# Routing stage of a fused transformer kernel: chunk 0's logits, choice and slots first on each engine, the row statistics of chunk 3 behind them

## The chip, the cores and the metric

The kernel runs on one NeuronCore of a Trainium2 chip. TensorE (PE; PEld are its weight loads), VectorE (DVE), ScalarE (ACT), GpSimd (POOL) and the DMA queues of SyncE (SP) run lists of instructions of their own and meet at semaphores. The metric is the device time of one execution in microseconds (us); three runs of the kernel before gave 1239.8 to 1245.31, median 1242.03.

## What is computed

```python
x = x + _layernorm(_L0_attn_ref(_layernorm(x, axis=-1), ...), axis=-1)   # attention, x is (8, 256, 256)
x = x + _layernorm(_L0_ffn_ref(_layernorm(x, axis=-1), ...), axis=-1)    # mixture of experts
x = x + _layernorm(_L1_attn_ref(_layernorm(x, axis=-1), ...), axis=-1)   # state space layer
x = x + _layernorm(_L1_ffn_ref(_layernorm(x, axis=-1), ...), axis=-1)    # dense layers

def _L0_ffn_ref(x, router_w, router_bias, wg, wu, wd, swg, swu, swd):
    logits = flat @ router_w                                     # 2048 tokens, 64 experts
    _, topk_idx = jax.lax.top_k(logits + router_bias, 4)
    ...
    routed = jnp.einsum('ne,nef,efd->nd', comb, g * u, wd)       # four experts a token
    shared = jnp.einsum('nsh,shd->nd', sg * su, swd)             # two experts that see every token
    return (routed + shared).reshape(b, t, d)
```

The change lies in the first part of the second line: the normalised rows, the logits, the choice of four experts and the places ("slots") to which each token's row is sent.

## The kernel before

The 2048 tokens lie in 16 tiles of 128, and four tiles make a chunk: chunks 0 to 3. The attention stage ends with `y`, the attention's output. For chunks 0 and 1 it has itself normalised `y`, added it to `x`, and written the normalised `rows`. For chunks 2 and 3 this is left to the routing stage (`stage_route`, from line 869), which runs these lists:

- VectorE (from line 1280): `statistics(src, kind, g)` takes mean and variance of four tiles. `low_parts(g)` makes the low half of the transposed rows, `choose(g)` ranks the logits and marks four experts, `tables(n)` sums how many rows each expert has, `find_slots(g)` writes `slots`, which releases the scatters of chunk g. `add(g)` adds the normalised `y` to `x`. `product(n)` and `low(n)` belong to step n of the shared experts, 16 steps, four for each chunk.
- GpSimd (from line 950): a "deviation" is a power of -0.5 and a product, by `spread`, with `deviations(kind, g)` for y or x. Then 64 indirect DMAs, one for each tile and choice, send rows of 128 tokens from `rows` to `slots_in` in DRAM (line 971). Two may be in flight (`IN_FLIGHT`): number n waits until n - 2 has landed. `BEFORE_ROWS` says ahead of which number a deviation is done.
- TensorE (from line 1058): `turn(g)` transposes rows, `score(g)` makes logits (24 products of 64 columns), `place_chunk(g)` counts and ranks once `choose(g)` is done. `up(n)` and `down(n)` are the shared experts' products; the second half of `up(n)` waits for `product(n - 1)`, `down(n)` for `low(n)`. Chunk 0's four steps come first, then `turn(2)`, which needs the accumulators back.
- ScalarE (from line 1131): `high_parts(0)`, `high_parts(1)`, `scale_y(2)`, `scale_y(3)`, `step(0)`, `step(1)`, `fill_rows(2)`, `step(2)`, `fill_rows(3)`, `step(3)`, `take(0)`. `scale_y(g)` waits for y's deviation of chunk g, `fill_rows(g)` for x's; `step(n)` makes the gate (a SiLU) of step n and rounds its product; `take(0)` empties the accumulators (`y_out`).
- SyncE (line 941): waits until all scatters have landed and loads the rows of the first experts from `slots_in`, on which the next stage begins.

The waits on deviations go by number: `rstd_ready` counts in the order of `NORM_ORDER`, (y, 2), (y, 3), (x, 2), (x, 3). The orders are written out by hand.

Of the kernel before, what the change touches and what calls it, by code (L numbers as in the profile page):

```python
# [24 lines left out]
FE, TOPK = 64, 4  # L25
# [6 lines left out]
NCH = TOK // CHUNK  # L32
TPC = CHUNK // P
# [51 lines left out]
def linker(eng, sem):  # L85

    n = [0]

    def link(ins):
        n[0] += 1  # L90
        ins.then_inc(sem, 1)
        eng.wait_ge(sem, n[0])

    return link
# [15 lines left out]
def flat(ap):  # L110
    return ap.rearrange("p a b -> p (a b)")
# [304 lines left out]
OF_Y, OF_X = range(NORMS)  # L416
# [5 lines left out]
EARLY_NORMS = 2  # L422
# [21 lines left out]
def spread(nc, link, norms, kind, tiles):  # L444

    part = slice(tiles.start, tiles.stop)
    rstd = norms["rstd"][:, kind, part]
    link(nc.gpsimd.tensor_tensor(rstd, norms["var"][:, kind, part], norms["power"][:], ALU.pow))
    return nc.gpsimd.tensor_tensor(norms["shift"][:, kind, part], norms["negmean"][:, kind, part], rstd, ALU.mult)
# [360 lines left out]
PARTIES = PARTY[-1] + 1  # L810
N_SEEN, N_OVER, N_LIMIT, N_BASE = range(4)
NORM_ORDER = [(OF_Y, 2), (OF_Y, 3), (OF_X, 2), (OF_X, 3)]
BEFORE_ROWS = {4: 2, 8: 3}
SLOT_TILES = NE + OVER
SLOT_ROWS = SLOT_TILES * P
BLANK = 8
# [52 lines left out]
def stage_route(chip, x, rows, norms, xh, xl, y, ident, xs, t, ahead, router, ins):  # L869
# [10 lines left out]
    with ExitStack() as ctx:  # L880
# [45 lines left out]
        slots_ready, scattered = chip.sem("slots_ready"), [chip.kept_sem("scattered") for _ in range(IN_FLIGHT)]  # L926
# [4 lines left out]
        def tiles(g):  # L931
            return slice(g * TPC, (g + 1) * TPC)
# [5 lines left out]
        def normed(kind, g):  # L938
            return NORM_ORDER.index((kind, g)) + 1

        with nc.Block() as block:
            @block.sync
            def _(sp):
                for q in range(AHEAD):
                    load_experts(sp, ahead, ins, q, ahead["w_loaded"][q])
                for done in scattered:
                    sp.wait_ge(done, NT * TOPK // IN_FLIGHT * 16)
                for g in range(DEEP):
                    load_quad(sp, xs, ahead, g)

            @block.gpsimd
            def _(pool):
                chip.clear_old()
                link = linker(pool, pool_link)

                def deviations(kind, g):
                    pool.wait_ge(var_ready, normed(kind, g))
                    spread(nc, link, norms, kind, range(g * TPC, (g + 1) * TPC)).then_inc(rstd_ready, 1)

                for g in range(EARLY_NORMS, NCH):  # L960
                    deviations(OF_Y, g)
                for g in range(NCH):
                    pool.wait_ge(slots_ready, g + 1)
                    for i in range(g * TPC, (g + 1) * TPC):
                        for k in range(TOPK):
                            n = i * TOPK + k
                            if n in BEFORE_ROWS:
                                deviations(OF_X, BEFORE_ROWS[n])
                            if n >= IN_FLIGHT:
                                pool.wait_ge(scattered[n % IN_FLIGHT], n // IN_FLIGHT * 16)  # L970
                            nc.gpsimd.indirect_dma_start(  # L971
                                out=xs[:, :], out_offset=bass.IndirectOffsetOnAxis(slots[:, i, k:k + 1], 0),
                                in_=rows[:, i, :], in_offset=None).then_inc(scattered[n % IN_FLIGHT], 16)

            @block.tensor
            def _(pe):
                def turn(g):
                    for b in (2 * g, 2 * g + 1):
                        if g >= EARLY_NORMS:
                            pe.wait_ge(xn_ready, b - 2 * EARLY_NORMS + 1)  # L980
                        if b >= len(turned):
                            pe.wait_ge(lo_ready, b - len(turned) + 1)
                        for n in range(2):
                            for k in range(KD):
                                last = nc.tensor.transpose(turned[b % len(turned)][:, k, n * P:(n + 1) * P],
                                                           rows[:, 2 * b + n, k * P:(k + 1) * P], ident[:])
                        last.then_inc(xn_turned, 1)
# [3 lines left out]
                def score(g):  # L991
                    if g >= 2:
                        pe.wait_ge(logits_out, g - 1)
                    for i in range(TPC):
                        if i % 2 == 0:
                            pe.wait_ge(lo_ready, 2 * g + i // 2 + 1)
                        t0 = (g * TPC + i) * P
                        for m, (a, w, k) in enumerate(parts):
                            last = nc.tensor.matmul(logits[g % 2][:, i, :], a[:, k, t0:t0 + P], w[:, k, :],
                                                    start=(m == 0), stop=(m == len(parts) - 1))  # L1000
                    last.then_inc(logits_done, 1)
# [23 lines left out]
                def place_chunk(g):  # L1025
                    pe.wait_ge(chosen_done, g + 1)
                    count(g)
                    rank(g)
# [28 lines left out]
                    last.then_inc(down_done, 1)  # L1057

                turn(0)
                turn(1)  # L1060
                score(0)
                place_chunk(0)
                score(1)
                pe.wait_ge(logits_out, 1)
# [89 lines left out]
            def _(dve):  # L1154
                link = linker(dve, chain)

                def statistics(src, kind, g):
                    for i in range(g * TPC, (g + 1) * TPC):
                        last = nc.vector.bn_stats(norms["stats"][:, kind, i, :], src[:, i, :])
                    link(last)  # L1160
                    measure(nc, link, norms, kind, range(g * TPC, (g + 1) * TPC)).then_inc(var_ready, 1)

                def add(g):
                    dve.wait_ge(y_scaled, g - EARLY_NORMS + 1)
                    link(nc.vector.tensor_tensor(flat(x[:, tiles(g), :]), flat(x[:, tiles(g), :]),
                                                 flat(y[:, tiles(g), :]), ALU.add))

                def low_parts(g):
                    for b in range(2 * g, 2 * g + 2):
                        dve.wait_ge(hi_ready, b + 1)  # L1170
                        nc.vector.tensor_tensor(xl[:, :, b * S:(b + 1) * S], turned[b % len(turned)],
                                                xh[:, :, b * S:(b + 1) * S].bitcast(F32),
                                                ALU.subtract).then_inc(lo_ready, 1)

                def choose(g):
                    dve.wait_ge(logits_done, g + 1)
                    link(nc.vector.tensor_tensor(ranked[:, tiles(g), 0:NE], logits[g % 2],
                                                 bias[:].unsqueeze(1).broadcast_to([P, TPC, NE]), ALU.add))
                    nc.vector.tensor_copy(logit[:, tiles(g), :], logits[g % 2]).then_inc(logits_out, 1)
                    for i in range(g * TPC, (g + 1) * TPC):  # L1180
                        last = nc.vector.max(best[:, i, :], ranked[:, i, :])
                    link(last)
                    for i in range(g * TPC, (g + 1) * TPC):
                        last = nc.vector.match_replace(left[:, i, :], best[:, i, :], ranked[:, i, :], -BIG)
                    link(last)
                    nc.vector.tensor_tensor(chosen[:, tiles(g), :], ranked[:, tiles(g), 0:NE], left[:, tiles(g), 0:NE],
                                            ALU.not_equal).then_inc(chosen_done, 1)
# [73 lines left out]
                def product(n):  # L1261
                    dve.wait_ge(silu_done, n + 1)
                    dve.wait_ge(up_done, n + 1)
                    if n >= 2:
                        dve.wait_ge(lo_done, n - 1)
                        dve.wait_ge(hi_done, n - 1)
                    nc.vector.tensor_tensor(prod[:, n % 2, :], gate[:, n % 2, :], pu[:], ALU.mult).then_inc(prod_done, 1)
# [9 lines left out]
                    product(n)  # L1277
                    low(n)

                statistics(y, OF_Y, 2)  # L1280
                nc.vector.memset(ranked[:, :, NE:], BIG)
                link(nc.vector.memset(scan[:], 0.0))
                set_tables()
                low_parts(0)
                low_parts(1)
                statistics(y, OF_Y, 3)
                choose(0)
                add(2)
                tables(0)
                find_slots(0)  # L1290
                choose(1)
                product(0)
                statistics(x, OF_X, 2)
                low(0)
# [1712 lines left out]
```

## Time and profile before

| | before |
|---|---|
| median of three runs | 1242.03 us |
| profiled execution | 1239.46 us |
| its span | 1237.6 us |
| busy of the span: PE, DVE, ACT, POOL | 1106.0, 869.7, 637.7, 378.7 us |
| routing stage | about 220 to 346 us |

The span is measured from the first instruction to the last; the profiled execution's own time has 1.9 us more around it. The chain of waits that the profile follows back from the last instruction covers only the last part of the kernel, so for the routing stage the timelines of the engines have to be read.

### The profile page before, as it was taken

The page shows a single profiled execution, that of the slowest core. Times are in us where ns is not written, and L with a number is a line of the kernel's source. Part 1 is how long each engine was busy: PE and PEld are TensorE (multiplying, and loading weights), DVE is VectorE, ACT ScalarE, POOL GpSimd, SP SyncE. Part 2 cuts the span into 40 slices and gives each one's busy share as a digit, 9 for nine tenths or more (in the row PEclk, how much of TensorE's full clock was granted, in tenths as well). Part 3 has the DMA queues.
Part 4 walks back from the last instruction along what each step waited for, and adds up shares of the span by engine and source line. Part 5 has one row for each costly group of instructions (what it writes and reads, how often), then busy time and mean ns, then how long its engine had stood idle before and what let it go on. Part 6 is the DMA issues. An engine that isn't in the chain of part 4 may idle for free. (4 is left out here: it accounts for less than half of the span.)

```text
span 1237.6 us, 31648 instructions
## 1 busy us (share of the span) xinstructions
PE 1106.0 (89%) x12161; PEld 909.0 (73%) x12161; DVE 869.7 (70%) x2188; ACT 637.7 (52%) x1449; POOL 378.7 (31%) x545
## 2 busy tenths in 40 slices
PE   6779998788989994777699999999999999999996
PEld 5646775677778994555467888888888888888896
DVE  6767896867946678776476677667766776664675
ACT  4644545233333784666545555555455545553665
POOL 3521222266700065761263036102610262000121
PEclk9979999678999997778899999999999999999998
DMA  6838883222289896551523243223342342232001
GB/s 173 248 123 218 237 219 138 117 80 90 86 329 419 294 316 206 165 184 77 144 83 95 87 125 108 87 87 121 113 157 91 112 124 87 87 104 87 5 18 52
DMA packets 77986, 176.17 MB, mean 142 GB/s; under 512 B 12614, under 2 KB 26182, under 8 KB 75270
## 3 DMA queue, kind: packets, MB, share of 16 engines
q1 hardware_dynamic: 71564, 157.09, 39.1%
q0 software_dynamic: 6272, 17.05, 4.5%
q8 instruction: 97, 1.59, 0.5%
q14 instruction: 53, 0.43, 0.1%
HBM read 112.82 MB, written 61.08 MB: 141 GB/s over the span
## 5 line engine op out<-in xcount | busy, mean ns | idle before, releaser
L2395 ACT ACTIVATE decay<-masked,negcum 128x128 f32<-128x128 f32 x512 | 163.1, 391 | 102.1 <-DVE mixT L2459 102.1
L2303 PE MATMUL joint<-xh,w_high 128*128 128x512 f32 x512 | 209.2, 409 | 2.0 <-POOL wl L2239 2.0
L2303 PE MATMUL joint<-xl,w_high 128*128 128x512 f32 x512 | 200.2, 391 | 0.0
L2303 PE MATMUL joint<-xh,wl 128*128 128x512 f32 x512 | 199.9, 390 | 0.0
L2507 DVE COPY cT<-joint 128x512 f32<-128x512 f32 x128 | 88.3, 689 | 85.8 <-PE joint L2303 85.4
L2413 ACT ACTIVATE bT<-joint 128x512 f32<-128x512 f32 x128 | 76.6, 599 | 130.4 <-PE joint L2303 130.4
L2459 DVE TENSOR_TENSOR mixT<-pcb,decay 128x512 f32<-128x512 f32 x128 | 82.4, 685 | 53.8 <-PE pcb L2319 53.8
L2236 POOL TENSOR_TENSOR w_high<-w_in,none 128x512 fp32r<-128x512 f32 x32 | 34.7, 1084 | 262.3 <-DMA w_in<-in_w_bc 253.2
L2303 PEld LDWEIGHTS joint<-xh,w_high 128*128 128x128 f32 x512 | 96.2, 188 | 23.7 <-POOL wl L2239 2.4
L2303 PEld LDWEIGHTS joint<-xh,wl 128*128 128x128 f32 x512 | 96.1, 188 | 20.7
L2303 PEld LDWEIGHTS joint<-xl,w_high 128*128 128x128 f32 x512 | 96.3, 188 | 17.0
L2449 DVE TENSOR_TENSOR masked<-cumrow,mask 128x512 f32<-128x512 f32 x128 | 101.9, 796 | 0.1
L699 ACT ACTIVATE probT<-pst 128x384 f32<-128x384 f32 x128 | 60.2, 490 | 65.2 <-PE pst L630 61.9
L2319 PEld LDWEIGHTS pcb<-cT,bT 128*32 128x32 f32 x4096 | 79.4, 110 | 11.7 <-issue 11.7
L2319 PE MATMUL pcb<-cT,bT 128*32 128x128 f32 (+3 forms) x4096 | 84.7, 234 | 0.0
L971 POOL DMA_INDIRECT slots_in<-rows,slots x64 | 66.3, 1036 | 41.8 <-DMA slots_in<-rows,slots 20.4
L2468 DVE TENSOR_TENSOR cS<-cT,grown 128x256 f32<-128x256 f32 x128 | 62.4, 488 | 13.4 <-ACT grown L2400 1.3
L1602 DVE TENSOR_TENSOR rows<-gate,pgu 64x512 f32<-64x512 f32 x64 | 44.2, 691 | 26.4 <-ACT gate L1557 25.4
L738 DVE CUSTOM_DVE_ANT_0 masked<-ps,reach 128x128 f32<-128x128 f32 x128 | 36.7, 286 | 24.5 <-PE ps L614 23.3
L740 DVE CUSTOM_DVE_ANT_0 masked<-ps,reach 128x256 f32<-128x256 f32 x128 | 53.7, 419 | 0.0
L2400 ACT ACTIVATE grown<-cumrow 128x256 f32<-128x256 f32 x128 | 51.6, 403 | 0.0
L2251 POOL COPY y<-val 32x128 f32<-32x128 f32 x128 | 43.2, 337 | 7.6
(369 smaller groups left out, 2698.7 us busy)
## 6 DMA issues: line engine op xcount, KB each, us to landing
cumrow<-ssm_cum SPq DMA_DIRECT2D x128, 256.0 KB, 3.3
slots_in<-blank SPq DMA_DIRECT2D x16, 1024.0 KB, 5.3
rows<-slots_in SPq DMA_DIRECT2D x32, 512.0 KB, 5.9
slots_out<-spare SPq DMA_DIRECT2D x32, 512.0 KB, 4.8
weights<-in_expert_quads SPq DMA_DIRECT2D x16, 768.0 KB, 9.0
w_in<-in_w_bc SPq DMA_DIRECT2D x32, 256.0 KB, 3.7
qk_parts<-parts SPq DMA_DIRECT2D x32, 192.0 KB, 2.8
stack<-qk_parts SPq DMA_DIRECT2D x32, 192.0 KB, 5.1
```

The lines of the kernel that those rows point to most:

```text
L699: nc.scalar.activation(probT[:, n % HELD, :], pst[n % T_BANKS][:, 0:3 * P], ACT.Exp).then_inc(exped, 1)
L740: nc.vector.tensor_tensor_reduce(dst[:, P:3 * P], src[:, P:3 * P], reach[:], accum_out=highest[:, u % 2, j, 1:2], **form).then_inc(maxed, 1)
L971: nc.gpsimd.indirect_dma_start(out=xs[:, :], out_offset=bass.IndirectOffsetOnAxis(slots[:, i, k:k + 1], 0), in_=rows[:, i, :], in_offset=N ...
L2303: last = nc.tensor.matmul(bank[:], w[:, j, col:col + P], a[:, k, c * CHUNK:(c + 1) * CHUNK], start=(m == 0), stop=(m == len(parts) - 1))
L2319: last = nc.tensor.matmul(pcb[n % 2][at:at + KEY, reach], bT[:, n % B_BUFS, keys], cT[:, n % 2, reach], start=True, stop=True, skip_group_ ...
L2395: last = nc.scalar.activation(decay[:, n % 2, o], masked[:, n % 2, o], ACT.Exp, bias=negcum[:, c * TPC + i, head:head + 1])
L2400: nc.scalar.activation(grown[:, n % 2, :, :], row[:, :, P:S], ACT.Exp).then_inc(grown_out, 1)
L2413: nc.scalar.activation(bT[:, n % B_BUFS, :], pbT[:], ACT.Copy).then_inc(b_out, 1)
L2449: nc.vector.tensor_tensor(masked[:, n % 2, :].rearrange("p (q l) -> p q l", l=S), cumrow[:, n % CUMS, :].rearrange("p (q l) -> p q l", l=S ...
L2459: nc.vector.tensor_tensor(mixT[:, n % KEEP, :], pcb[n % 2][:], decay[:, n % 2, :], ALU.mult).then_inc(mix_out, 1)
L2468: nc.vector.tensor_tensor(cS[:, n % KEEP, :, :], second, grown[:, n % 2, :, :], ALU.mult).then_inc(c_scaled, 1)
L2507: nc.vector.tensor_copy(cT[:, n % 2, :], pcT[:]).then_inc(c_out, 1)
```

## The change

It alters the order of work in the routing stage on three engines, and nothing else.

- VectorE: the memsets and tables come first, then `low_parts(0)`, `statistics(y, 2)`, `choose(0)`, `low_parts(1)`, `tables(0)`, `find_slots(0)`; then `statistics(y, 3)`, `choose(1)`, `add(2)`, and from `product(0)` on the list is as before.
- TensorE: `score(0)` comes ahead of `turn(1)`.
- GpSimd: y's deviation of chunk 2 is done before the wait for chunk 0's slots, y's of chunk 3 ahead of scatter 4, x's of chunks 2 and 3 ahead of scatters 8 and 12 (before: y's both first, x's ahead of 4 and 8).

ScalarE's and SyncE's lists are as before.

```diff
-BEFORE_ROWS = {4: 2, 8: 3}
+BEFORE_ROWS = {0: (OF_Y, 2), 4: (OF_Y, 3), 8: (OF_X, 2), 12: (OF_X, 3)}
...
-                for g in range(EARLY_NORMS, NCH):
-                    deviations(OF_Y, g)
                 for g in range(NCH):
-                    pool.wait_ge(slots_ready, g + 1)
                     for i in range(g * TPC, (g + 1) * TPC):
                         for k in range(TOPK):
                             n = i * TOPK + k
                             if n in BEFORE_ROWS:
-                                deviations(OF_X, BEFORE_ROWS[n])
+                                deviations(*BEFORE_ROWS[n])
+                            if n % (TPC * TOPK) == 0:
+                                pool.wait_ge(slots_ready, g + 1)
                             if n >= IN_FLIGHT:
...
                 turn(0)
+                score(0)
                 turn(1)
-                score(0)
                 place_chunk(0)
...
-                statistics(y, OF_Y, 2)
                 nc.vector.memset(ranked[:, :, NE:], BIG)
                 link(nc.vector.memset(scan[:], 0.0))
                 set_tables()
                 low_parts(0)
+                statistics(y, OF_Y, 2)
+                choose(0)
                 low_parts(1)
-                statistics(y, OF_Y, 3)
-                choose(0)
-                add(2)
                 tables(0)
                 find_slots(0)
+                statistics(y, OF_Y, 3)
                 choose(1)
+                add(2)
                 product(0)
```

## Rows read from the trace of the kernel before

**Rows 1.** GpSimd's timeline: start us, us, engine, line, what, [idle before <-releaser].
```profile
229.47 0.20 POOL L449 TENSOR_TENSOR norm_shift<-norm_negmean,norm_rstd 128x4 f32<-128x4 f32 x1
241.67 1.22 POOL L971 DMA_INDIRECT slots_in<-rows,slots  x1 [12.01 <-DVE slots L1251]
...
246.91 1.26 POOL L448 TENSOR_TENSOR norm_rstd<-norm_var,norm_power 128x4 f32<-128x4 f32 x1
248.25 0.21 POOL L449 TENSOR_TENSOR norm_shift<-norm_negmean,norm_rstd 128x4 f32<-128x4 f32 x1
...
289.34 1.05 POOL L971 DMA_INDIRECT slots_in<-rows,slots  x1 [0.30 <-DMA slots_in<-rows,slots]
293.08 0.95 POOL L971 DMA_INDIRECT slots_in<-rows,slots  x1 [2.69 <-DVE slots L1251]
...
339.82 0.96 POOL L971 DMA_INDIRECT slots_in<-rows,slots  x1 [0.44 <-DMA slots_in<-rows,slots]
```

**Rows 2.** SyncE's timeline at the end of the stage.
```profile
342.31 6.26 SPq L862 DMA_DIRECT2D rows<-slots_in  x4
```

**Rows 3.** VectorE's timeline, from the stage's start to `low(3)`.
```profile
220.70 1.41 DVE L1159 BATCH_NORM_STATS2 norm_stats<-y 128x6 f32<-128x256 f32 x4 [0.33 <-PEq L523]
...
222.75 0.11 DVE L1281 MEMSET ranked<- 128x64 f32 x1
...
223.55 1.29 DVE L1171 TENSOR_TENSOR xl<-acc,xh 128x512 fp32r<-128x512 f32 x2
...
230.91 1.22 DVE L1165 TENSOR_TENSOR x<-x,y 128x1024 f32<-128x1024 f32 x1
232.16 0.22 DVE L1198 TENSOR_TENSOR table<-table,counts 128x64 f32<-128x64 f32 x1
...
241.28 0.42 DVE L1177 TENSOR_TENSOR ranked<-pg,router_bias 128x256 f32<-128x256 f32 x1
...
243.98 0.68 DVE L1267 TENSOR_TENSOR prod<-gate,pu 128x512 f32<-128x512 f32 x1
...
249.23 0.69 DVE L1267 TENSOR_TENSOR prod<-gate,pu 128x512 f32<-128x512 f32 x1 [0.84 <-PE pu L1034]
...
253.43 0.69 DVE L1267 TENSOR_TENSOR prod<-gate,pu 128x512 f32<-128x512 f32 x1 [0.92 <-ACT gate L1125]
...
259.71 0.68 DVE L1267 TENSOR_TENSOR prod<-gate,pu 128x512 f32<-128x512 f32 x1
...
263.23 0.69 DVE L1273 TENSOR_TENSOR hl<-prod,hh 128x512 fp32r<-128x512 f32 x1
```

**Rows 4.** ScalarE's timeline.
```profile
221.37 1.08 ACT L1096 ACTIVATE xh<-acc 128x512 fp32r<-128x512 f32 x2 [9.17 <-PE acc L985]
...
239.86 0.60 ACT L1125 ACTIVATE gate<-pg 128x512 f32<-128x512 f32 x1 [6.79 <-PE pg L1034]
...
250.49 2.07 ACT L454 ACTIVATE rows<-x,norm_shift,norm_rstd 128x256 f32<-128x256 f32 x4
...
306.06 1.28 ACT L1125 ACT_TABLE_LOAD   x1
307.35 0.60 ACT L1125 ACTIVATE gate<-pg 128x512 f32<-128x512 f32 x1
```

**Rows 5.** Busy time by stretch; behind POOL's: granted clock, DMA share, GB/s.
```profile
224.00:227.00 3.00, 2.71 (x25) 2.71 (x25) 2.82 (x7) 2.02 (x5) 0.16 (x1) 1.00 1.01 418
227.00:232.00 5.00, 1.87 (x14) 1.67 (x14) 4.83 (x24) 2.83 (x7) 1.20 (x2) 0.50 0.58 242
```

**Rows 6.** TensorE's timeline: products of the logits.
```profile
224.70 0.28 PE L999 MATMUL pu<-router_wh,xh 128*128 128x64 f32 x1
...
226.82 0.28 PE L999 MATMUL pu<-router_wl,xh 128*128 128x64 f32 x1
...
231.79 0.40 PE L999 MATMUL pg<-router_wh,xh 128*128 128x64 f32 x1
...
236.70 0.40 PE L999 MATMUL pg<-router_wh,xl 128*128 128x64 f32 x1
```

## The prediction

> **What bounds the kernel now.** I read four views of the routing stage, in this order. First GpSimd's timeline. The 64 row scatters are the stage's last work: number 0 starts at 241.67 us, number 31 at 289.34, then GpSimd idles 2.69 us for the slots of chunk 2, and numbers 32 to 63 run from 293.08 to 339.82, a pitch of 1.51 us [rows 1]. SyncE waits for the last landing and loads the first expert rows at 342.31 [rows 2]. So the end hangs on when chunk 2's slots are written, not on when the first scatter starts: chunks 0 and 1 have idle time behind them.
>
> Then, what makes chunk 2's slots late. TensorE must give the accumulators of chunk 0's shared experts back (`y_out`) before `turn(2)`, so the chain runs back over `down(3)` to the DVE step `low(3)`, at 263.23 [rows 3]. Behind it the order is fixed: `low(3)`, `down(3)`, `take(0)`, `turn(2)`, `score(2)`, `choose(2)`, `choose(3)`, `tables(2)`, `find_slots(2)`, 32 scatters. A shift of `low(3)` is a shift of the stage's end, one for one.
>
> Last, what `low(3)` hangs on. In front of it VectorE works nearly without a pause from 220.70: the pauses marked are 0.84 us before `product(1)` and 0.92 us before `product(2)` [rows 3]. ScalarE is idle for much of it; it takes the first gate at 239.86 after waiting 6.79 us for TensorE [rows 4]. TensorE's clock is at its high level (1.00, 2.4 GHz) to 227 us and at the low one (0.50, 1.2 GHz) behind it [rows 5].
>
> **The change part by part.** The instructions are the same ones; none is added. Only orders change, on three engines. ScalarE's order is not touched, and there the price lies: its list still says `scale_y(2)`, `scale_y(3)`, `step(0)`. `scale_y(3)` waits for chunk 3's y power, which so far came at 229.5 + 0.2, long before the gate [rows 1]. I follow the new times.
>
> *VectorE's front.* `statistics(y, 2)` costs 2.05 us (220.70 to 222.75), the memsets and `set_tables` 0.80 (to 223.55) [rows 3]. Now the memsets go first, to 221.50. `low_parts(0)` needs ScalarE's first `xh`, 221.37 + 0.60 [rows 4], so it starts at 222.05 and, at 0.61 each (as `low_parts` ran), ends at 223.25. `statistics(y, 2)` then lasts to 225.3. Its power is done beside `choose(0)` on an idle GpSimd, so `scale_y(2)` and `add(2)` are never late.
>
> *TensorE's front.* `score(0)` starts after the first low part, 222.75. It is 24 products of 64 columns. At the high clock their pitch is 0.112 us (224.70 to 226.82 in 19 steps), at the low one 0.2135 (231.79 to 236.70 in 23) [rows 6]. Bounds, with the last one's own length: all high 222.75 + 23 x 0.112 + 0.28 = 225.6; all low 222.75 + 23 x 0.2135 + 0.40 = 228.1. The clock fell once while `score(0)` ran, although 12 transposes and 4 more preceded the fall; now 8 transposes and a pause of 1 us do, and narrow products. I take the fall after the first six products: 222.75 + 6 x 0.112 + 17 x 0.2135 + 0.40, the logits are there at 227.5. That is nearer to the low end, because the engine does less in front of it than in the rows where the high level was kept.
>
> *Choice and slots of chunk 0.* `choose` costs 2.70 us (241.28 to 243.98), `tables(0)` and `find_slots(0)` 9.12 together (232.16 to 241.28) [rows 3]. `choose(0)` ends at 230.2; `low_parts(1)` follows, 1.2 us, to 231.4, and covers `place_chunk(0)` on TensorE as `add(2)` did (1.25 us, 230.91 to 232.16). If that cover were gone the wait would be about 1 us. Slots: 231.4 + 9.1 = 240.5 instead of 241.28. So the first scatter is 0.8 us earlier, at 240.9 (2.7 us earlier if the clock holds).
>
> *The power of y 3 behind four scatters.* `statistics(y, 3)` now follows the slots: 240.5 to 242.55. Then `choose(1)` to 245.25 and `add(2)` to 246.5. GpSimd meets `deviations(y, 3)` as number 4 is due. From number 0 to that point is 246.91 - 241.67 = 5.24 us, power and shift take 1.55 (246.91 to 248.25 + 0.21) [rows 1]: 240.9 + 5.24 + 1.55 = 247.7. Then ScalarE: `scale_y(3)` 2.07 us as the four of `fill_rows(2)` take, the table load 1.29 (306.06 to 307.35), the gate and the step to VectorE 0.63 [rows 4]. Together 251.7. `product(0)` was at 243.98 [rows 3]: it is **7.7 us later**, and VectorE, ready at 246.5, idles 5.2 us. Queued behind the wait on ScalarE are `step(0)`, `step(1)`, `fill_rows(2)` and all that follows; behind VectorE's wait `statistics(x, 2)` and everything to `low(3)`; TensorE's `up(1)` stops halfway, since its second half waits for `product(0)`.
>
> On the table load a rule and a row differ. The row of the switch after the exponential shows 1.28 us, and the gate starts 0.01 us behind it [rows 4]. The Trainium skill ("ScalarE: Activation LUTs", What ACT_TABLE_LOAD costs) adds a drain and gives 2.66 us for each switch; by it the sum would be 1.4 us more. The row is this case's, and I go by it.
>
> *What is won back.* Between `product(0)` and `product(1)` 0.84 us of waiting for TensorE falls away, since `up(1)`'s gate half is long done: 4.4 us instead of 5.25, so `product(1)` is at 256.1, 6.9 late [rows 3]. The 0.92 us ahead of `product(2)` stay, because ScalarE still puts `fill_rows(2)` (2.07) between: 4.2 us on, 260.3. The x powers come at scatter 8 and 12 instead of 4 and 8. x 2 is measured at 251.7 + 0.6 + 2.05 = 254.3, when GpSimd has made four scatters at 1.51 behind 247.7 (253.7); its power is done at 255.9, before `fill_rows(2)` can start at some 257.4. x 3 is due four scatters later, at 261.9, and done at 263.5; `fill_rows(3)` then lasts to 265.6 and the gate of `step(3)` to 266.2, while `product(3)` is due at 260.3 + 6.3 = 266.6 (253.43 to 259.71): hidden, with 0.4 us left. If four scatters took 2 us more, it would cost 1.6.
>
> *Chunks 0 and 1 on GpSimd.* One power more between scatters is 1.5 us in a queue that must wait for chunk 1's and chunk 2's slots anyway: nothing.
>
> *Sum.* From `product(2)` to `low(3)` nothing changes (9.8 us, 253.43 to 263.23), so `low(3)` is at 270.1, **6.9 us late**, and so is the stage. The stages behind it are the same. The profiled execution took 1239.46 us for a span of 1237.6, and would become 1246.4. It lay 2.6 us under the median of 1242.03; on the median I forecast 1248.9. A half per cent, 6.2 us, is about what a measurement of this kernel can tell from no change.
>
> **The rivals.**
> A. *The clock holds through `score(0)`.* Then the logits are there at 225.6, the slots at 225.6 + 2.7 + 1.2 + 9.1 = 238.6, and all behind them is 1.9 us earlier than in the sum: `low(3)` 5.0 us late, 1247.0. For it: all 8 transposes and the first 20 products ran high in the kernel before [rows 6]. Against: the same narrow products then fell to the low level, and the work ahead of them is a third less. The Trainium skill ("TensorE: Matmul & The Clock Gate", HAM oscillation) says that pauses between bursts lose the high clock, which speaks for the forecast and against A; the fall behind 227 us in the trace [rows 5] agrees.
> B. *TensorE becomes late.* It idles while VectorE waits; if it is at the low clock in `up(1)` to `up(2)`, 18 wide products and 12 of `down(0)` at twice their time put `product(2)` 1 to 2.7 us later. With 2.5: 1251.4.
> C. *Faster: the scatter queue is the bound from the first one on.* Then the first scatter's lead of 2.7 us less the extra power's 1.5 is won: 1240.8, and with that power hidden in a pause 1239.3. It needs slots of chunk 2 before scatter 31 ends. Against it stands GpSimd's wait of 2.69 us [rows 1]; it decides only if `low(3)` is not held up by the gate, as it would with y 3's power before the first scatter.
> D. *The stall is absorbed:* 3 us or less are left of it, because `low(3)` to chunk 2's slots runs at another mix of clock levels (the scores at the high one throughout are worth 1.7 us) and ScalarE's part is shorter: 1244.5.
>
> **How the numbers follow.** Forecast 0.50, A 0.26, B 0.12, C 0.04, D 0.08. Predicted time 1248.9. Range 1244.5 to 1252.5: from D's value to B's with 1 us for the median of a few runs. Slower by over 0.5% (beyond 1248.2): 0.7 of the forecast, a quarter of A, B nearly all, 0.54. Within 0.5%: the rest of the forecast and of A, D, half of C, 0.43. Faster by over 0.5% needs more than C gives as I price it: 0.03.
>
> **What would show it.** In the new trace: first scatter at 239 to 241; y 3's power at 244 to 246, behind four scatters; ScalarE idle up to it, then `scale_y`, the table load and the gate in one row, the gate's idle naming no TensorE; VectorE's wait of about 5 us ahead of `product(0)`, put down to ScalarE; `low(3)` near 270; GpSimd's wait ahead of scatter 32 grown from 2.7 us to 5 or more; SyncE's first load near 349. The prediction is wrong if the gate comes before 248, if `low(3)` moves and scatter 32 does not, or if scatter 32 moves and the last landing does not.

## The result, and the profile after

| | before | changed |
|---|---|---|
| median of 7 runs each | 1243.06 us | 1251.36 us (1248.25 to 1254.32) |
| ratio to before | 1 | 1.0065, 95% interval 1.0049 to 1.0081 |
| profiled execution, its span | 1239.46, 1237.6 | 1252.56, 1250.6 |

The change costs 8.3 us by the medians. The forecast was 6.9 us more and a time of 1248.9.

The routing stage of the changed execution begins 1.04 us earlier (VectorE's first instruction at 219.66, before at 220.70, [rows 3]), so all comparisons of places below count from the stage's start. VectorE's timeline of the changed kernel answers [rows 3]; the columns are start, duration, engine, line, operation, and in brackets the idle time ahead and what ended it.

```profile
219.66 0.11 DVE L1279 MEMSET ranked<- 128x64 f32 x1 [0.37 <-PEq L523]
...
221.44 1.47 DVE L1170 TENSOR_TENSOR xl<-acc,xh 128x512 fp32r<-128x512 f32 x2 [1.01 <-ACT xh L1095]
...
227.55 0.42 DVE L1176 TENSOR_TENSOR ranked<-pu,router_bias 128x256 f32<-128x256 f32 x1 [2.64 <-PE pu L998]
...
245.29 1.22 DVE L1164 TENSOR_TENSOR x<-x,y 128x1024 f32<-128x1024 f32 x1
251.81 0.69 DVE L1266 TENSOR_TENSOR prod<-gate,pu 128x512 f32<-128x512 f32 x1 [5.30 <-issue]
...
256.27 0.69 DVE L1266 TENSOR_TENSOR prod<-gate,pu 128x512 f32<-128x512 f32 x1
...
260.53 0.69 DVE L1266 TENSOR_TENSOR prod<-gate,pu 128x512 f32<-128x512 f32 x1 [0.98 <-ACT gate L1124]
...
266.88 0.69 DVE L1266 TENSOR_TENSOR prod<-gate,pu 128x512 f32<-128x512 f32 x1 [0.23 <-ACT gate L1124]
...
270.41 0.69 DVE L1272 TENSOR_TENSOR hl<-prod,hh 128x512 fp32r<-128x512 f32 x1
```

The reader is to see the 5.30 us ahead of the first product. The profile calls it "issue", but ScalarE's timeline says what it is:

```profile
229.82 2.06 ACT L454 ACTIVATE y<-y,norm_shift,norm_rstd 128x256 f32<-128x256 f32 x4
247.74 2.07 ACT L454 ACTIVATE y<-y,norm_shift,norm_rstd 128x256 f32<-128x256 f32 x4 [15.86 <-POOL norm_shift L449]
249.83 1.28 ACT L1124 ACT_TABLE_LOAD   x1
251.13 0.60 ACT L1124 ACTIVATE gate<-pg 128x512 f32<-128x512 f32 x1
```

ScalarE stands still for 15.86 us, released by GpSimd; `scale_y(3)`, the table load and the gate follow without a gap, and 0.08 us behind the gate VectorE goes on. The gate itself waits for nothing: TensorE's last product for it ended at 239.2, some 12 us before the gate. GpSimd's timeline, which answers [rows 1], has the power that is waited for, behind four scatters:

```profile
240.97 1.22 POOL L970 DMA_INDIRECT slots_in<-rows,slots  x1 [14.69 <-DVE slots L1250]
...
246.24 1.19 POOL L448 TENSOR_TENSOR norm_rstd<-norm_var,norm_power 128x4 f32<-128x4 f32 x1
247.50 0.21 POOL L449 TENSOR_TENSOR norm_shift<-norm_negmean,norm_rstd 128x4 f32<-128x4 f32 x1
...
293.54 0.96 POOL L970 DMA_INDIRECT slots_in<-rows,slots  x1 [0.30 <-issue]
300.69 0.96 POOL L970 DMA_INDIRECT slots_in<-rows,slots  x1 [6.20 <-DVE slots L1250]
...
348.75 0.96 POOL L970 DMA_INDIRECT slots_in<-rows,slots  x1 [0.30 <-DMA slots_in<-rows,slots]
```

and SyncE's, which answers [rows 2]:

```profile
351.24 6.34 SPq L862 DMA_DIRECT2D rows<-slots_in  x4
```

Where the time went, counted from each stage's start (start to place, in us):

| place | before | changed | later by | forecast |
|---|---|---|---|---|
| first scatter | 20.97 | 21.31 | 0.34 | -0.8 |
| `product(0)` | 23.28 | 32.15 | 8.87 | 7.7 |
| `product(1)` | 28.53 | 36.61 | 8.08 | 6.9 |
| `low(3)` | 42.53 | 50.75 | 8.22 | 6.9 |
| scatter 32 | 72.38 | 81.03 | 8.65 | 6.9 |
| SyncE's first load | 121.61 | 131.58 | 9.97 | 6.9 |

From the start of the kernel the load is 8.93 us later, since the stage began 1.04 earlier. The span of this execution is 13.0 us longer than that of before, which is 4.7 more than the medians differ: the further stages add 4.1 in this pair of executions. The main loop of the state space stage, whose code is unchanged, starts 12.8 us later (SyncE's `w_in` loads at 607.53 and 620.31), so nearly all of that came up ahead of it. I didn't follow it further. The medians, of seven executions each, differ by 8.3 us only, so I don't count it to the change.

### The profile page after: what moved, and what is told of

Read it like the earlier page. It is cut to its first block and busy times, and to the rows that moved or that the text cites. A ratio compares the mean times of both kernels' runs of the same rounds, so it can differ in the third digit from the quotient of the medians.

```text
span 1250.6 us, 31647 instructions
## 1 busy us (share of the span) xinstructions
PE 1114.1 (89%) x12161; PEld 915.2 (73%) x12161; DVE 870.3 (70%) x2188; ACT 637.7 (51%) x1449; POOL 383.1 (31%) x545
## 5 line engine op out<-in xcount | busy, mean ns | idle before, releaser
L1481 PE MATMUL pt<-ident,rows 128*128 128x128 f32 x256 | 37.0, 288 | 10.5 <-PEq L941 6.1
```

## The experiments

All times are medians of runs of the kernel beside runs of the kernel before on the same chip, and the ratio is to those. "Stage" is the time from VectorE's first instruction of the routing stage to TensorE's first transpose of the next (before: 125.66 us), and `low(3)` counts from the same start (before: 42.53); both are of the one profiled execution. Where two runs of the table are compared with each other, the noise given is the 95% interval of the difference of their ratios.

| kernel | median, before beside it | ratio, 95% interval | `low(3)` | stage |
|---|---|---|---|---|
| changed | 1251.36, 1243.06 | 1.0065, 1.0049 to 1.0081 | 50.75 | 135.62 |
| y power at scatter 4, x's at 8 and 12, nothing else | 1252.59, 1243.07 | 1.0083, 1.0065 to 1.0102 | 52.69 | 138.89 |
| y power at scatter 8, x's at 12 and 14, nothing else | 1257.60, 1242.59 | 1.0107, 1.0078 to 1.0135 | 55.93 | 139.35 |
| `score(0)` first, alone | 1248.12, 1243.07 | 1.0046, 1.0029 to 1.0062 | 48.95 | 133.05 |
| changed, `turn(1)` first | 1248.48, 1242.59 | 1.0045, 1.0027 to 1.0063 | 49.03 | 134.85 |
| changed, y power at scatter 2 | 1249.63, 1242.59 | 1.0057, 1.0036 to 1.0077 | 46.96 | 129.50 |
| changed, gate ahead of `scale_y(3)` | 1246.37, 1243.07 | 1.0026, 1.0012 to 1.0041 | 47.05 | 129.15 |
| changed, y 3 measured in the gap | 1244.61, 1243.07 | 1.0015, 1.0001 to 1.0029 | 46.89 | 128.84 |
| the same, x powers at 4 and 8 | 1242.65, 1242.39 | 1.0001, 0.9985 to 1.0018 | 43.93 | 127.58 |
| before, `low(3)` earlier | 1241.68, 1242.39 | 0.9988, 0.9971 to 1.0006 | 42.41 | 127.09 |
| before, four scatters in flight | 1239.81, 1242.39 | 0.9985, 0.9973 to 0.9997 | 41.91 | 123.88 |
| both of these | 1239.31, 1242.39 | 0.9970, 0.9951 to 0.9990 | 40.05 | 122.46 |

The last column holds more than the edits. From `low(3)` to scatter 32 TensorE makes the logits of chunks 2 and 3, and that stretch took 27.5 us where its granted clock was 0.81 in the mean (gate ahead of `scale_y(3)`), 29.9 at 0.67 (before), 30.3 at 0.71 (changed), 32.5 at 0.63 (`turn(1)` first) and 33.6 at 0.60 (y power at scatter 4). `low(3)` is the better measure of an edit in one trace, and the medians that of the whole.

The theory is that the change's price is one wait: ScalarE meets `scale_y(3)` ahead of the first gate, and its input, y's power of chunk 3, now stands behind the slots of chunk 0 and four scatters on GpSimd. Rival 1 puts the price on TensorE (the order of `score(0)` and `turn(1)`, and the low clock), rival 2 on the longer queue of scatters.

### The late power alone

```diff
 # kernel before
-BEFORE_ROWS = {4: 2, 8: 3}
+BEFORE_ROWS = {4: (OF_Y, 3), 8: (OF_X, 2), 12: (OF_X, 3)}
...
-                for g in range(EARLY_NORMS, NCH):
-                    deviations(OF_Y, g)
+                deviations(OF_Y, 2)
...
-                                deviations(OF_X, BEFORE_ROWS[n])
+                                deviations(*BEFORE_ROWS[n])
```

> The kernel before with one part of the change alone: y's power of chunk 3 is done ahead of scatter 4 (x's ahead of 8 and 12), all other orders as before. Theory: ScalarE's scale_y(3), and the first gate queued behind it, wait for that power. It starts at 246.9 us, and with 1.5 for power and shift, 2.07 for scale_y(3), 1.29 for the table load and 0.63 for the gate product(0) comes at 252.4 instead of 243.98; 0.84 of that is won back ahead of product(1). The kernel takes 7.5 us more than before, 6 to 9. Rival 1, the order on TensorE with its low clock is the price: no difference. Rival 2, the additional power in the scatter queue: 1.5 us more.

Measured: 9.5 us more than before, a little over the range. VectorE's timeline of this run:

```profile
221.96 1.41 DVE L1158 BATCH_NORM_STATS2 norm_stats<-y 128x6 f32<-128x256 f32 x4 [0.32 <-PEq L523]
...
231.67 0.42 DVE L1176 TENSOR_TENSOR ranked<-pu,router_bias 128x256 f32<-128x256 f32 x1 [1.64 <-PE pu L998]
...
255.72 0.69 DVE L1266 TENSOR_TENSOR prod<-gate,pu 128x512 f32<-128x512 f32 x1 [8.20 <-ACT gate L1124]
```

The statistics are taken as early as before, and still the whole price is there: 8.20 us ahead of `product(0)`, this time put down to the gate. x's powers moved too, as in the change, but the first gate doesn't wait for them; what they add in this trace is a wait of 0.40 us ahead of `product(3)`. Rivals 1 and 2, with 0 and 1.5 us, are out as main causes. The profiled execution, 4.6 us above the run's median, has two more delays, both with TensorE at its low clock although nothing of its order was changed: the logits of chunk 0 are waited for for 1.64 us (first eight transposes 1.94 us, against 1.07 in the kernel before), and the stretch behind `low(3)` is the longest of all. Whether they are in the median of 9.5 us too isn't shown.

The same with the power four scatters later:

```diff
-BEFORE_ROWS = {4: 2, 8: 3}
+BEFORE_ROWS = {8: (OF_Y, 3), 12: (OF_X, 2), 14: (OF_X, 3)}
```

> The kernel before with y's power of chunk 3 ahead of scatter 8 (x's ahead of 12 and 14), all other orders as before: the suspected wait made longer by four scatters against the run with the power ahead of scatter 4. Theory: four scatters at 1.4 us, 5.5 us more than that run, which was 9.5 more than before: 15 more than before (13 to 17). Rival, the wait is not the price, and the power only has to be in the queue: as that run, 9.5.

Measured: 15.0 us more by the medians, as expected; by the ratio 13.3 (9.7 to 16.8).

```profile
260.64 0.69 DVE L1266 TENSOR_TENSOR prod<-gate,pu 128x512 f32<-128x512 f32 x1 [13.56 <-ACT gate L1124]
```

VectorE's wait ahead of `product(0)` grew from 8.20 to 13.56 us, by 5.4 for four scatters, and so did the time from the first scatter to `product(0)`, from 10.59 to 15.95. The wait scales with the place of the power. That the kernel's time grows by as much is not shown: between these two runs the ratios differ by 3.0 us with a noise of about 4, and the stages of the two traces by 0.5, since the stretch behind `low(3)` took 33.6 us there and 29.1 here.

### The place of the power in the changed kernel

```diff
-BEFORE_ROWS = {0: (OF_Y, 2), 4: (OF_Y, 3), 8: (OF_X, 2), 12: (OF_X, 3)}
+BEFORE_ROWS = {0: (OF_Y, 2), 2: (OF_Y, 3), 8: (OF_X, 2), 12: (OF_X, 3)}
```

> The changed kernel with y's power of chunk 3 ahead of scatter 2 instead of 4. Its variance is there at 242.6 us, scatter 1 is issued at 243.5. Theory: the power starts at 243.5 instead of 246.24, product(0) is 2.7 us earlier: 2.5 us less than the changed kernel, 5.8 more than before (4.5 to 7). Rival 2 (one more power in the queue, wherever it is): as the changed kernel.

Measured: 7.0 us more than before, at the edge of the range; the step down from the changed kernel is 1.3 by the medians, within the noise of both. The trace has it clearly: VectorE's wait falls from 5.30 to 2.36 us, which is 2.9 for an expected 2.7.

```profile
249.83 0.69 DVE L1266 TENSOR_TENSOR prod<-gate,pu 128x512 f32<-128x512 f32 x1 [2.36 <-issue]
```

The mechanism holds in the trace. That the time follows is shown only by steps that are clear of noise: the late power alone above, and the two edits further on that take the wait away.

### TensorE's order alone

```diff
 # kernel before
                 turn(0)
-                turn(1)
                 score(0)
+                turn(1)
```

> The kernel before with one part of the change alone: score(0) ahead of turn(1) on TensorE. Theory: VectorE has statistics of y to do while the logits are made, so even at the low clock they come no more than 1 us later than in the kernel before: 0 to 1 us more. Rival 1, that the order on TensorE is the price of the change: 5 us more or above.

Measured: 5.1 us more, a miss, and as a number it is what rival 1 was given. The trace says why:

```profile
230.62 0.69 DVE L1171 TENSOR_TENSOR xl<-pg,xh 128x512 fp32r<-128x512 f32 x1 [6.37 <-ACT xh L1096]
```

I had forgotten `low_parts(1)`. In the kernel before it stands ahead of `statistics(y, 3)` and `choose(0)` on VectorE, and it needs `turn(1)`; behind 24 products it comes 6.37 us late. The changed kernel has `low_parts(1)` behind `choose(0)`, where it waits for nothing. So by the trace this part of the change has that price only without VectorE's half, and the run doesn't speak for rival 1 in the changed kernel. The test that does undoes TensorE's order in the changed kernel:

```diff
 # changed kernel
                 turn(0)
-                score(0)
                 turn(1)
+                score(0)
```

> The changed kernel with TensorE's order put back (turn(1) ahead of score(0)), VectorE's and GpSimd's as changed. Theory: the logits come up to 1 us later, the first scatter and the wait behind it too: 0 to 1 us more than the changed kernel, 8 to 9 more than before. Rival 1 (score(0) first is the price): most of the 8 us go.

Measured: 5.9 us more than before, so some 2.4 less than the changed kernel, where I expected up to 1 more. Those 2.4 us are not clear of noise (the ratios differ by 2.5 us, with a noise of about 3), but the trace gives rival 1 a small part of the price. The wait for the gate is unchanged, the wait for the logits is not:

```profile
227.90 0.42 DVE L1176 TENSOR_TENSOR ranked<-pu,router_bias 128x256 f32<-128x256 f32 x1 [0.95 <-PE pu L998]
...
252.15 0.69 DVE L1266 TENSOR_TENSOR prod<-gate,pu 128x512 f32<-128x512 f32 x1 [5.30 <-issue]
```

0.95 us instead of 2.64. TensorE's timelines show it, first of the changed kernel, then of this one:

```profile
219.61 1.94 PE L984 MATMUL acc<-ident,rows 128*128 128x128 f32 x8 [1.05 <-PEq L523]
222.18 0.42 PE L998 MATMUL pu<-router_wh,xh 128*128 128x64 f32 x1 [0.63 <-DVE xl L1170]
...
227.11 0.40 PE L998 MATMUL pu<-router_wh,xl 128*128 128x64 f32 x1
```

```profile
221.65 1.94 PE L984 MATMUL acc<-ident,rows 128*128 128x128 f32 x8 [1.05 <-PEq L523]
223.38 1.06 PE L984 MATMUL pg<-ident,rows 128*128 128x128 f32 x4
224.23 1.02 PE L984 MATMUL acc<-ident,rows 128*128 128x128 f32 x4
224.99 0.30 PE L998 MATMUL pu<-router_wh,xh 128*128 128x64 f32 x1
```

Both begin at the low level. With all 16 transposes in a row the clock is high when the products of the logits start (0.99 granted from 225 to 227.8); with eight, a pause and narrow products it stays low through all 24 (0.50 granted from 219 to 228). So in this pair, `score(0)` ahead of `turn(1)` made the logits 1.68 us later from the stage's start (7.89 against 6.21), though they are asked for first. `low(3)` is 1.72 us earlier for it in this run. One execution of each is profiled, and how often each pattern occurs is open.

### The gate freed from the power

```diff
 # changed kernel
-                scale_y(3)
                 step(0)
+                scale_y(3)
```

> The changed kernel, but ScalarE does step(0) ahead of scale_y(3), so the first gate no longer stands behind the power of y of chunk 3. Theory: product(0) comes as VectorE is ready, some 5.3 us earlier; the wait is then met once more at scale_y(3) ahead of add(3) and the second gate, but hidden to a part: product(1) is 5 us earlier than in the changed kernel. 5 us less than the changed kernel, which is 3 us more than before (1.5 to 4.5). Rivals 1 and 2 (TensorE's order, the queue of scatters): as the changed kernel, 8 us more than before.

Measured: 3.3 us more than before, 5.0 less than the changed kernel, as expected. The gate comes at 241.60, as soon as TensorE has its input, and VectorE does `product(0)` without a wait. But the trace has a new wait, further on:

```profile
241.60 0.60 ACT L1124 ACTIVATE gate<-pg 128x512 f32<-128x512 f32 x1 [6.02 <-PE pg L1033]
...
248.95 0.69 DVE L1266 TENSOR_TENSOR prod<-gate,pu 128x512 f32<-128x512 f32 x1
...
259.71 0.69 DVE L1266 TENSOR_TENSOR prod<-gate,pu 128x512 f32<-128x512 f32 x1 [2.87 <-ACT gate L1124]
```

Swapping two calls on an engine that the change did not touch takes away more than half of its price, clear of noise (by the ratios 4.8 us, with a noise of 2.7). That settles the main cause against both rivals.

### The statistics of chunk 3 in the gap

VectorE waits 2.64 us for the logits in the changed kernel, and `statistics(y, 3)` takes 2.0:

```diff
 # changed kernel (VectorE, then GpSimd)
                 statistics(y, OF_Y, 2)
+                statistics(y, OF_Y, 3)
                 choose(0)
...
                 find_slots(0)
-                statistics(y, OF_Y, 3)
...
+                for g in range(EARLY_NORMS, NCH):
+                    deviations(OF_Y, g)
                 for g in range(NCH):
...
-BEFORE_ROWS = {0: (OF_Y, 2), 4: (OF_Y, 3), 8: (OF_X, 2), 12: (OF_X, 3)}
+BEFORE_ROWS = {8: (OF_X, 2), 12: (OF_X, 3)}
```

> The changed kernel, but the statistics of y of chunk 3 are taken ahead of choose(0), in VectorE's wait of 2.64 us for the logits, and both powers of y are done ahead of the first scatter; score(0) stays first on TensorE. Theory: the first gate no longer waits; VectorE reaches product(0) 1.6 us later than before, counted from the stage's start, and wins 0.84 back behind it: 0.8 us more than before, -0.5 to 2. Rival 1 (TensorE's order): still some 8 us more. Rival 2 (queue of scatters): 1.5 us less than the changed kernel.

Measured: 1.5 us more than before, 6.8 less than the changed kernel, with `score(0)` first and the low clock still there (logits at 7.89 us from the start, as in the changed kernel). What is left is again a wait on a power, now x's, which stands behind eight scatters:

```profile
253.41 2.08 ACT L454 ACTIVATE rows<-x,norm_shift,norm_rstd 128x256 f32<-128x256 f32 x4 [3.51 <-POOL norm_shift L449]
```

VectorE's wait ahead of `product(2)` is 4.16 us here. In the changed kernel the longer stall in front hid the late place of x's powers. The next run gives these their old place:

```diff
 # kernel of the run above
-BEFORE_ROWS = {8: (OF_X, 2), 12: (OF_X, 3)}
+BEFORE_ROWS = {4: (OF_X, 2), 8: (OF_X, 3)}
```

> The kernel with chunk 3's y statistics in the gap, and in addition x's powers ahead of scatters 4 and 8 again, as in the kernel before, instead of 8 and 12. In the run without this, VectorE waited 4.16 us ahead of product(2) for the gate that ScalarE does behind fill_rows(2), which waits for x's power. Theory: the price of a power's late place is paid wherever ScalarE's list meets it; here 3.3 us go: 3.3 less than the kernel with y's statistics in the gap, 1.8 less than before (-3.5 to 0). Rival, only y's power counts: no difference from the kernel with the gap filled, 1.5 more than before.

Measured: 0.3 us more than before (ratio 1.0001), 1.3 to 1.7 less than without this edit, where 3.3 were expected; the upper edge of the range is just missed. The step is within the noise of the two runs (about 2.7), so the time doesn't decide between theory and rival; the trace does. The wait ahead of `product(2)` fell from 4.16 to 0.55, but one of 0.96 stands ahead of `product(3)` (0.40 without this edit), because x's power of chunk 3 came behind a scatter that waited 2.29 us for a landing. With all powers early again, the new orders on VectorE and TensorE cost nothing that can be measured, and bring nothing.

### What does set the end

```diff
 # kernel before
                 product(3)
-                find_slots(1, lambda: low(3))
+                low(3)
+                find_slots(1)
```

> The kernel before, but VectorE does low(3) at once behind product(3), ahead of find_slots(1). It tests that low(3) sets the stage's end one for one. Theory: low(3) can run at 261.0 instead of 263.23, so down(3), take(0), turn(2) and chunk 2's slots come 2.2 us earlier; scatter 31 ends at 290.4, so scatter 32 can follow at 290.9: 2.2 us less than before (1.5 to 2.5). Rival, the queue of scatters as a whole is the bound: no difference.

Measured: 0.7 us less, interval -3.6 to +0.7 (by the ratio 1.5 less). Neither answer is excluded by the time. The trace shows why the gain is small: GpSimd no longer waits for chunk 2's slots at all. These are scatters 31 and 32:

```profile
293.16 0.97 POOL L971 DMA_INDIRECT slots_in<-rows,slots  x1 [0.35 <-DMA slots_in<-rows,slots]
295.05 0.96 POOL L971 DMA_INDIRECT slots_in<-rows,slots  x1 [0.91 <-DMA slots_in<-rows,slots]
```

Scatter 32 waits for a landing; VectorE had written its slots at 293.5, ahead of the end of scatter 31. Behind the first scatter no bracket names slots up to here, so the queue is the bound, and this execution's first scatter was late (23.2 us from the start, before 20.97), again with a wait of 1.64 us for logits at the low clock. By [rows 1], then, some 2.69 us are all that an earlier `low(3)` could win before the queue takes over; no run shows that gain.

```diff
 # kernel before
-IN_FLIGHT = 2
+IN_FLIGHT = 4
```

> The kernel before with four scatters in flight instead of two. A scatter's pitch of 1.5 us has about 0.35 us of waiting for a landing in it. Theory: scatters 32 to 63 take 1.27 us each, 41 instead of 48, but the shared experts' last product and take(3) end at 342.7 and hold the next stage, so 2.5 us less than before (1 to 3.5) and not 7. Rival, landings queue in the DMA engines: no difference.

> The kernel before with low(3) ahead of find_slots(1) and four scatters in flight. Theory: the two ends of the stage, the last scatter and the last shared product, both hang on low(3), so the gains add: 4.5 us less than before (3 to 6). Rival, they overlap: as the better one alone, 2.5 less.

Measured: 2.6 and 3.1 us less than before by the medians; by the ratios 1.9 (0.4 to 3.4) and 3.7 (1.2 to 6.1). Both are in their ranges, and the version with both edits is faster than both kernels. Its stage is 3.2 us shorter in its trace. That the two gains add is not shown: the intervals overlap.

With four in flight the number came and its reason did not: the scatters' pitch (start to start) was to fall from 1.51 us to 1.27, and from 291.25 to 336.87 it is 1.47. Of the 1.8 us by which the stage is shorter in this trace, 1.1 lie in that pitch; most of the rest is `low(3)`, 0.6 earlier. The groups of scatters in the second half (columns: count, busy us, mean ns, idle before and releasers), kernel before, then four in flight:

```profile
L971 POOL DMA_INDIRECT slots_in<-rows,slots x32 | 34.3, 1073 | 16.1 <-DMA slots_in<-rows,slots 9.1 <-issue 4.3 <-DVE slots L1251 2.7
```

```profile
L971 POOL DMA_INDIRECT slots_in<-rows,slots x32 | 37.1, 1160 | 15.0 <-issue 9.4 <-DVE slots L1251 5.5
```

The 9.1 us put down to landings are gone, but 5.1 of them come back as "issue": 0.30 us stand ahead of every scatter, whoever is named. So the time between scatters fell by 4.0 us, from 13.4 to 9.4, and the scatters themselves take 2.8 more. Why they do is the last point below.

## Why the prediction came out as it did

**The mechanism: right, and shown.** The wait of `scale_y(3)` on y's power, and the first gate queued behind it on an engine whose order wasn't changed, is the price. It was made by its cause alone (9.5 us of time), grew with it in the trace (5.4 us of wait for four scatters), and went with it (5.0 us of time for swapping two calls, 6.8 for measuring y 3 early). The trace gives the terms as they were summed: 5.27 us from the first scatter to the power (forecast 5.24), 1.5 to the end of the shift, then 4.1 for `scale_y(3)`, table load and gate (forecast 3.99). The table load is again 1.28 us with the gate right behind it, so the sum by the row was right, and the drain of 1.38 us that the Trainium skill ("ScalarE: Activation LUTs", What ACT_TABLE_LOAD costs) adds does not show here either.

**VectorE's wait**: 5.30 us, forecast 5.2. The releaser was not named as expected: the profile says "issue".

**TensorE's front: the term that was too small.** I took six products at the high clock and the logits 6.8 us behind the stage's start. They came at 7.89, beyond even my bound for a clock low throughout (7.4): the clock was low from the first transpose on, so that the first product started 2.52 us behind the stage's start and not 2.05. The low level was already there when the stage began, which the rows of before couldn't tell, and it made 1.1 of the 1.3 us by which `low(3)` came later than forecast. The first scatter was therefore 0.34 us later than before, not 0.8 earlier. That it stands at 240.97 and `low(3)` at 270.41, as forecast, is chance: the stage began 1.04 us earlier. Rival A, with the clock high throughout, did not occur in the profiled execution; of four more runs built on the changed kernel with `score(0)` ahead, two (y 3 in the gap; x powers back) were low through all 24 products, and two (gate first; power at scatter 2) began high and fell after two to three and after seven products. The Trainium skill ("TensorE: Matmul & The Clock Gate", HAM oscillation) has idle gaps lose the high clock; here it was narrow products without a gap that didn't regain it. Nor did the rows of before bear that rule out as plainly as I wrote: there the level fell behind 20 products without a gap, the last pause, of 2.09 us, lying ahead of the transposes in front of them.

**What was won back**: 0.79 us ahead of `product(1)`, forecast 0.84. Ahead of `product(3)` I had 0.4 us of slack; there was a wait of 0.23, because on the way to scatter 12 one scatter waited 1.91 us for a landing.

**From `low(3)` to the end**: not one for one. My sum had nothing for TensorE's clock there, and only rival D priced it, at 1.7 us towards faster; in the traces of the experiments this stretch varies with it from 27.5 us (0.81 granted) to 33.6 (0.60). Scatter 32 moved 0.43 us more, with a wait of 1.15 ahead of `product(4)` for TensorE at its low clock, and scatters 32 to 63 had a pitch of 1.55 instead of 1.51, 1.3 us in all. In this execution the stage's earlier beginning offset 1.04 us of it.

**Rival B** (TensorE late): did not occur; `product(2)` waited 0.98 for the gate, as the 0.92 before. **Rival C** (queue the bound) was right on what would be needed: it is the state of the kernel with an earlier `low(3)`, in which GpSimd's wait is gone. **Rival D** (the stall absorbed) did not occur: all of it is left at `low(3)` (8.2 us) and at the end.

**The number**: 8.3 us for 6.9, in the range, and slower beyond a half per cent as held likeliest.

## What to carry to other kernels

When work is moved on some engines, read the list of every engine that is not moved: the price here was an unchanged line, in front of an unrelated gate, on a mostly idle engine. A small operation that is placed "between" the items of a slow queue costs its consumer all items ahead of it. And ask what a chunk's earlier start can move at all: GpSimd idled for chunk 2's slots ([rows 1]), so an earlier chunk 0 had nothing to give. That last point is read from the rows; no run has an earlier chunk 0 and nothing else.

## What the runs showed of the hardware beyond that

- TensorE's clock at the same point of the same code differs between executions. The first eight transposes of the stage took 1.07 us (before, four in flight) or 1.94 us (power at scatter 4, the same order on TensorE). A level read from one trace is not a property of the order.
- A scatter that starts while VectorE works on two operands in SBUF is held up until VectorE is done. With four in flight the common duration is 0.96 us, but beside operations on 128x1024 elements it is 1.55:

```profile
313.94 1.22 DVE L1332 TENSOR_TENSOR moved<-place,last 128x1024 f32<-128x1024 f32 x1
...
314.44 1.55 POOL L971 DMA_INDIRECT slots_in<-rows,slots  x1 [0.30 <-issue]
...
315.80 1.22 DVE L1335 TENSOR_TENSOR moved<-moved,expd 128x1024 f32<-128x1024 f32 x1
316.29 1.56 POOL L971 DMA_INDIRECT slots_in<-rows,slots  x1 [0.30 <-issue]
```

  In the thirteen traces, from 288 us on, 104 scatters start with more than 0.4 us of such an operation still to go. Every one of them takes 0.96 us and the rest of the operation less 0.12 to 0.14. A reduction over as many elements, with one large operand, costs a scatter nothing; 23 start with more than 0.4 us of one to go, and each takes 0.96. From the trace of the changed kernel:

```profile
319.54 1.21 DVE L1325 TENSOR_REDUCE total<-expd 128x16 f32<-128x1024 f32 x1
...
320.04 0.96 POOL L970 DMA_INDIRECT slots_in<-rows,slots  x1 [0.30 <-issue]
```

  The Trainium skill ("SBUF — State Buffer", SBUF: two separate sides) has a VectorE operation with two inputs in SBUF hold, as a whole, a port that a GpSimd operation reading SBUF needs. The traces agree, down to the reduction that costs nothing; no run here tested it by an edit. Eleven scatters with four in flight are lengthened so, by 6.1 us together, which is why the pitch is 1.47 us and not 1.27.
